# First layer, projections and the first maximum units of a two-layer graph kernel put into one pass

## The reference

```
h = max(layernorm(x), 0)
adj_hat = adj + I;  d = (rowsum(adj_hat) + 1e-8) ** -0.5
x = x + relu((d[:, None] * adj_hat * d[None, :]) @ h @ weight)      # layer 0

h = max(layernorm(x), 0)                                             # layer 1
q, k, v = (h @ W.T).reshape(128, 3327, 8) for W in (Wq, Wk, Wv)
a = einsum('dnh,dmh->dnm', q, k) * 128 ** -0.5 + adj + adj
out = einsum('dnm,dmh->dnh', softmax(a, axis=2), v).reshape(3327, 1024)
x = x + out @ Wo.T
```

## Time and profile before

| | us |
|---|---|
| median of 3 executions | 15108.52 (15092.42 to 15110.36) |
| the profiled execution, its own time | 15109.94 |
| its span, first to last instruction | 15108.1 |
| VectorE busy in the span | 13914.9 (92%) |
| TensorE busy | 13957.0 (92%) |
| ScalarE busy | 13462.3 (89%) |
| mean granted TensorE clock | 0.973 |

### The profile page before, as it was taken

One profiled execution on the slowest core, in us unless ns is written; L12 is line 12 of the kernel. 1 busy time (PEld: TensorE's weight loads), 2 busy tenths in 40 slices (PEclk: granted clock), 3 DMA queues, 4 the chain that ended last, 5 costly groups with the idle time before them and its releaser, 6 DMA issues. The chain is left out here.

```text
span 15108.1 us, 432848 instructions
## 1 busy us (share of the span) xinstructions
PE 13957.0 (92%) x143755; PEld 4993.4 (33%) x143755; DVE 13914.9 (92%) x27486; ACT 13462.3 (89%) x30436; POOL 336.0 (2%) x887
## 2 busy tenths in 40 slices
PE   1747999999999999999999999999999999999996
PEld 1612333333333333333333333333333333333334
DVE  3249999999999999999999999999999999999972
ACT  0225999999999999999999999999999999999993
POOL 0020000000000000000000000000000000000000
PEclk9867999999999999999999999999999999999996
DMA  7755565655656565655656565655656565655542
GB/s 282 228 129 123 135 143 134 138 138 136 139 135 143 133 144 134 141 134 134 143 134 144 133 141 134 143 134 134 144 134 141 134 143 135 143 135 137 139 108 59
DMA packets 2075487, 2120.62 MB, mean 140 GB/s; under 512 B 818858, under 2 KB 1827761, under 8 KB 2063377
## 3 DMA queue, kind: packets, MB, share of 16 engines
q1 hardware_dynamic: 2069616, 2049.07, 56.1%
q10 hardware_dynamic: 3744, 44.30, 0.7%
HBM read 1927.37 MB, written 165.28 MB: 139 GB/s over the span
## 5 line engine op out<-in xcount | busy, mean ns | idle before, releaser
L927 DVE CUSTOM_DVE_ANT_0 X<-X,adj_row 128x832 f32<-128x832 f32 x13312 | 13304.5, 1048 | 93.1 <-PE X L961 49.6
L866 ACT ACTIVATE prob<-S 128x416 f32<-128x416 f32 x26624 | 11894.9, 517 | 386.1 <-PE S L983 201.0
L983 PE MATMUL S<-q_blk,k_res 52*128 52x416 f16 x26624 | 6865.5, 343 | 44.5 <-ACT S L855 11.1
L1004 PE MATMUL O<-prob,v_pad 128*32 128x208 f32 (+1 forms) x87376 | 6721.1, 388 | 2.6
L961 PE MATMUL X<-mk,mq 40*128 40x416 f16 x26624 | 6298.9, 346 | 369.5 <-DVE m_part L927 335.3
L983 PEld LDWEIGHTS S<-q_blk,k_res 52*128 52x128 f16 x26624 | 2216.7, 93 | 4256.1 <-ACT S L855 1457.9
L1004 PEld LDWEIGHTS O<-prob,v_pad 128*32 128x32 f32 x87376 | 1830.0, 108 | 2531.8 <-issue 2048.0
L961 PEld LDWEIGHTS X<-mk,mq 40*128 40x128 f16 x26624 | 1586.7, 93 | 2434.5 <-DVE m_part L927 1999.8
L855 ACT ACTIVATE S<-adj_key 128x416 f32<-128x416 f32 x3328 | 1752.7, 527 | 184.0 <-DMA adj_key<-adj_by_key 148.7
L927 DVE DVE_READ_ACCUMULATOR2_ANT m_part<- 128x1 f32 x13312 | 1876.8, 141 | 0.0
L350 PE MATMUL tr<-ident,row 128*128 128x128 f32 x676 | 106.4, 286 | 322.8 <-DVE hn L300 321.7
(11 more groups left out here) (90 smaller groups left out, 1458.0 us busy)
## 6 DMA issues: line engine op xcount, KB each, us to landing
adj_row<-adj_padded SPq DMA_DIRECT2D x1664, 416.0 KB, 3.9
adj_key<-adj_by_key SPq DMA_DIRECT2D x3328, 208.0 KB, 3.4
mk<-k_planes SPq DMA_DIRECT2D x1664, 104.0 KB
mk<-k_planes SPq DMA_DIRECT2D x1664, 52.0 KB
adj_padded<-row ACTq DMA_DIRECT2D x26, 1664.0 KB, 5.4
row<-adj_padded SPq DMA_DIRECT2D x26, 1664.0 KB, 7.8
adj_by_key<-aT SPq DMA_DIRECT2D x26, 1664.0 KB, 11.9
row<-in_adj SPq DMA_DIRECT2D x25, 1663.5 KB, 7.3
```

The lines of the kernel that those rows point to most:

```text
L866: nc.scalar.activation(prob[c % QR][:, d % 4, :], S[b][:, 0:WB], ACT.Exp, scale=2.0).then_inc(s_e[b], 1)
L927: nc.vector.tensor_tensor_reduce(out=x_, in0=x_, in1=adj_row[gi % 4][:].rearrange("p (a b) -> p a b", a=2), scale=1.0, scalar=LOW, op0=ALU ...
L983: nc.tensor.matmul(S[b][:, 0:WB], k_res[base:base + KR, d // 2, s * P:(s + 1) * P], q_blk[n % 2][base:base + KR, d // 2, :], start=False, ...
L1004: done = nc.tensor.matmul(O[32 * d:32 * d + 32, cols], v_pad[:, s, 4 * q + d, :], prob[born(j, q) % QR][:, d, cols], start=first, stop=Tru ...
```

## The change

- Block 1 and block 2 become one block with one pass over the row tiles, and it also runs the first EU = 160 maximum units, eight in each of the row tiles 4 to 23, one or two in each group of transposes (`units_at`).
- The degree pass goes from the last tile to the first, with RB = 3 row buffers. Nothing but columns 2496 to 3327 (the fourth piece of `max_bias`) is stored, to `adj_tail`. The last three tiles loaded stay for the pass; the others are loaded from adj a second time.
- In the pass, tile t is transposed and aggregated while tile t - 1 is updated, normed (`row_update`, `row_norm`, `row_turn`) and projected (`project`, `rest`). `pj` is one bank; each half of q, k and v passes through it in turn. q, k and v have two buffers each in SBUF.
- `max_bias` reads adj itself for the first three pieces and `adj_tail` for the fourth, and only the rows there are: 127 in the last tile.
- In block 3 ScalarE and GpSimd fill parts of `k_res`, ScalarE's queue issues the first group's value loads after its fill, and 24 maximum units precede the first score. The maximum helpers are unchanged otherwise, and so are the cycles, the spans and the output block.

```diff
+    EU = 160
+    XT = 4
+    RB = 3
-    adjp_t = dram("adj_padded", (NP, NP), fp32)
+    tail_t = dram("adj_tail", (NP, 2 * XC), fp32)
...
+            def max_bias(sp, x, gi):
+                c, t = gi // 2, gi % 2
+                r0 = x * 256 + t * P
+                n = min(P, N - r0)
+                src = adj[r0:r0 + n, c * 2 * XC:(c + 1) * 2 * XC] if c < 3 else adj_tail[r0:r0 + n, :]
+                sp.dma_start(adj_row[gi % 4][0:n], src).then_inc(s_ar[gi % 4], 16)
...
+                def units_at(t, g):
+                    if t < XT or t >= XT + EU // 8:
+                        return []
+                    u = 8 * (t - XT) + g + (g > 3)
+                    return [u, u + 1] if g == 3 else [u]
...
+                        for i in range(NT):                      # SP, degree pass
+                            t = NT - 1 - i
+                            if i >= RB:
+                                wait(sp, s_deg, i - RB + 1)
+                                wait(sp, s_tl[i % RB], 16 * (i // RB))
+                            load(t, False)
...
+                        for t in range(NT + 2):                  # SP, the pass
+                            if 1 <= t and t - 1 + RB < NT:
+                                ...
+                                load(t - 1 + RB, True)
+                            if 1 <= t <= NT:
+                                ...
+                                sp.dma_start(adjT_cols[:, :, (t - 1) * P:t * P], aT[(t - 1) % 2][:]).then_inc(s_at[(t - 1) % 2], 16)
+                            if t >= 2:
+                                ...                              # q, k and v of tile t - 2
...
+                        wait(sp, s_res, 2 * NT)
+                        sp.dma_start(x1_rows, xs[:]).then_inc(s_xo, 16)
+                        wait(sp, s_xo, 16)
...
+                        def project(t, i, h):                    # ScalarE
+                            e, s, cols = t - 1, (t - 1) % 2, slice(512 * h, 512 * h + 512)
+                            act.wait_ge(s_pj, 6 * e + 2 * i + h + 1)
+                            if i < 2:
+                                ...
+                                first = nc.scalar.activation((q_parts, k_parts)[i][s][:, 0, cols], pj[:], ACT.Copy)
+                                if i == 1:
+                                    first.then_inc(s_hi, 1)
+                                else:
+                                    nc.scalar.activation(q_parts[s][:, 2, cols], pj[:], ACT.Copy, scale=-1.0).then_inc(s_ng, 1)
+                            else:
+                                ...
+                                nc.scalar.activation(v_out[s][:, cols], pj[:], ACT.Copy).then_inc(s_vc, 1)
...
+                        for t in range(NT + 1):                  # VectorE
+                            for g in range(GN):
+                                ...                              # its copy of a transposed group
+                                if t >= 1:
+                                    if g == 2:
+                                        row_update(t - 1)
+                                    if g == 3:
+                                        row_norm(t - 1)
+                                    if g == 4:
+                                        row_turn(t - 1)
+                                    if g in (4, 5):
+                                        rest(t - 1, g - 4, 0)
+                                        rest(t - 1, g - 4, 1)
+                                for u in units_at(t, g):
+                                    sweep(dve, u)
...
+                        for t in range(NT + 1):                  # TensorE
+                            for g in range(GN):
+                                ...                              # transposes of group g
+                                if t >= 1 and g >= 4:
+                                    project(t, g - 4, 0)
+                                for u in units_at(t, g):
+                                    maximum(pe, 0, u, 1, END * NG)
+                                    maximum(pe, 0, u, 0, END * NG)
+                                if g == 0 and t >= 1:
+                                    products(t - 1, GN - 1)
+                                elif g and t < NT:
+                                    products(t, g - 1)
+                                ...
+                                if t >= 1 and g >= 4:
+                                    project(t, g - 4, 1)
...
+                        for r0, r1 in PIECES:                    # ScalarE, block 3
+                            nc.scalar.activation(k_res[32:64, :, r0 * P:r1 * P], zero.unsqueeze(2).to_broadcast((32, GH // 2, (r1 - r0) * P)), ACT.Copy, bias=MAX_STEP).then_inc(s_kz[0], 1)
+                        act.wait_ge(s_vz, 3)
+                        for piece in range(len(PIECES)):
+                            group_values(act, 0, piece)
...
-                    for u in range(LEAD):
-                        maximum(0, u, 1, END * NG)
-                        maximum(0, u, 0, END * NG)
+                        for u in range(EU, LEAD):
+                            maximum(pe, 0, u, 1, END * NG)
+                            maximum(pe, 0, u, 0, END * NG)
```

More of the change, by code:

```diff
@@ L529, in graph_layers_kernel @@
-        with ExitStack() as c4:
-            sb, pb, sem = open_(c4)
-            k_res = sb("k_res", [P, GH // 2, NP], fp16)
-            q_blk = [sb(f"q_blk{i}", [P, GH // 2, WB], fp16) for i in range(2)]
+        with ExitStack() as shared:
+            sb, pb, sem = open_(shared)
             mq = [sb(f"mq{i}", [P, GH, 2 * P], fp16) for i in range(3)]
@@ new lines, in sweep @@
+            def sweep(dve, v):
+                xh, u = v // 64, v % 64
+                gi, d = u // 8, u % 8
+                c, t = gi // 2, gi % 2
+                if d == 0:
+                    dve.wait_ge(s_ar[gi % 4], xh * 32 + 16 * (gi // 4 + 1))
+                dve.wait_ge(s_x[u % 2], xh * 32 + (u // 2 + 1))
+                x_ = X[u % 2][:, :, 0:XC]
+                nc.vector.tensor_tensor_reduce(out=x_, in0=x_, in1=adj_row[gi % 4][:].rearrange("p (a b) -> p a b", a=2),
+                                               scale=1.0, scalar=LOW, op0=ALU.add, op1=ALU.max,
+                                               accum_out=m_part[xh % 2][:, c, GH * t + d:GH * t + d + 1]).then_inc(s_t, 1)
+                if u == 1 and xh:
+                    max_reduce(dve, xh - 1)
+                if u == 6 and xh:
+                    max_turn(dve, xh - 1)
@@ new lines, in maximum @@
+            def maximum(pe, k, u, rg, end):
+                if u >= end:
+                    return
+                c, t, d = u // 16, u // 8 % 2, u % 8
+                x = u // 64
+                if rg == 1:
+                    if u % 64 == 0:
+                        pe.wait_ge(s_mq[x % 3], k * (64 * 13) + 64 * (x // 3 + 1))
+                    if u % 16 == 0:
+                        pe.wait_ge(s_mk[c % 3], k * (64 * 52) + 64 * (c // 3 + 1))
+                    if u >= 2:
+                        pe.wait_ge(s_t, k * SPAN + (u - 1))
+                base = 64 * rg
+                done = nc.tensor.matmul(X[u % 2][:, rg, 0:XC], mq[x % 3][base:base + XR, d, t * P:(t + 1) * P], mk[c % 3][base:base + XR, d, :], start=True, stop=True)
+                if rg == 0:
+                    done.then_inc(s_x[u % 2], 1)
```

1498 lines of the change are left out of this document (728 added, 770 removed).

## The result

The changed kernel takes 15162.17 us (median of 7 executions, 15151.7 to 15170.23), the kernel before 15110.36 (7 executions). The ratio is 1.0036, with a 95% interval from 1.0024 to 1.0048: slower by 52 us. I had forecast 14983 and faster. The profiled execution took 15170.23 us, its span is 15168.2, and its mean granted clock 0.968.

A forecast was written before the change was run, and what follows sets the result against it. The maximum units, with VectorE nearly full in the long stage, were taken to bound it. 15109.9 - 409 (early stages) + 25 (hand-over) + 257 (edge-row stalls) = 14983 us; range 14,690 to 15,230.

The forecast's parts named there:

- unit 160 runs at: Start of maximum unit 160, after which the schedule is unchanged except loads: 863 us instead of 1272, a gain of 409.
- hand-over, loss: Before the first scores: ScalarE's fill and 24 value loads delay its biases to 53 us, needed at 27.5; loss 25.
- edge rows, loss of 16 groups: Long stage: 127-row `adj_row` loads of the last tile stall VectorE 16 us a head group, 257 us in all.
- 4S + 3R + 2 = 89.5 us, wanted at 49 + 24.4 = 73.4: Landing of a head group's fourth 127-row load against its use, 24.4 us being the prefetch depth: 16 us late.
- R: Usual work per 16 units of the DMA engine carrying the 127 rows: 6.5 us taken, bounds 5 and 7.7.
- S = 17: Time in us of one 127-row load on one DMA engine, taken between estimates of 16 and 18.5.
- (b): Long stage: same queue, slower, 24 us or more a group; 25.7 gives 15,137, 34 gives 15,270 us; chance 0.18.
- (a): Long stage: the 127-row loads are hidden, no stall; 14726 us (14,640 to 14,830); chance 0.21.
- (c): Pass over row tiles stays at 1.2 GHz, 37 us a tile: 15,248 us with the stalls, 14,991 without; chance 0.08.
- Degree pass: First stage: two loads in flight, 6.2 us a tile, so TensorE starts at 188 us (bounds 150 and 220) against 321.4.
- The pass over the tiles: Merged row-tile pass: limited by `pj`'s chain of product, copies and rest; 26 us a tile with units, 655 in all.
- Odd pitch "at nothing": Row loads of the maximum units from adj, whose rows are 3327 elements: the odd pitch costs nothing.

The follow-up runs named there:

- experiments 1 to 4: Changed kernel's 127-row loads: split 112+15, 14705.32 us; 113+14, 15014.92; 122+5, 14701.87; 97+30, 14850.12; half the columns, 14704.99. Kernel before with 127-row loads: 15550.92.
- experiment 6: Changed kernel with the four 127-row loads of a head group issued whole from ScalarE's queue instead of SP's: 15174.25 us, ratio 1.0041.
- 113 rows: Changed kernel with each 127-row load of the last row tile split into 113 and 14 rows: 15014.92 us, ratio 0.9934.
- 97 rows: Changed kernel with each 127-row load of the last row tile split into 97 and 30 rows: 14850.12 us, ratio 0.9832.
- 112 + 15: Changed kernel with each 127-row load of the last row tile split into 112 and 15 rows: 14705.32 us, ratio 0.9729.
- experiment 5: Kernel before, first three column pieces read from adj at its odd pitch, all loads with 128 rows: 15109.52 us, ratio 1.0002.
- experiment 2: Kernel before, with only its last row tile's load cut from 128 to 127 rows, still from the padded copy: 15550.92 us, ratio 1.0289.

## Why the prediction was wrong, point by point

The terms, predicted and found; the last column is what each adds to 14983.

| term | predicted | found | difference |
|---|---|---|---|
| unit 160 runs at | 863 | 836 | -27 |
| hand-over, loss | 25 | 41.4 | +16 |
| edge rows, loss of 16 groups | 257 | 457 | +200 |

The sum is 15,172, against 15,170.2 of the profiled execution; with the 464 that the ratios give for the edge rows it would be 15,179.

**The step that failed** is the price of the edge rows, "4S + 3R + 2 = 89.5 us, wanted at 49 + 24.4 = 73.4: VectorE stalls 16 us a group". The mechanism was right: 127 rows ride on one engine (experiments 1 to 4), the stall lies where it was said, in three pieces at the end of each group. The size was too small, by 12.6 us a group, and from 24.7 us a group on the change is a loss: what it gains elsewhere is 1272 - 836 = 436 us, less the 41 of the hand-over, over 16. Two things make up the 12.6:

- **R, "I take 6.5", the other work of that engine.** From 97 to 127 rows the fourth load comes later by 97.6 - 82.3 = 15.3 us, so a row costs 15.3 / 30 / 4 = 0.128 us and 127 rows 16.2: S = 17 was close. The rest of the 97.6 is 32.8 = 3R + 2, so R is 10.3, above both bounds of the sum (5 and 7.7). I had left out half of `adj_row`'s part of the packet share (7.7) and gone lower still for packet time that counts waiting (6.5); not even the whole share, 9.5, was enough. Nor is it SP's order: in experiment 6, where each load was issued before the one ahead was down, the four landings (27.9, 20.2, 26.5, 25.3 us) leave 35.0 us beside 4 x 16.2. Of that 11.7 lie ahead of the first load, where the formula had 2, so "R" also holds work that was queued before the first. Which transfers the engine served in those 33 to 35 us no run resolves; that part of the cause stays open. R is what the formula leaves, from one group in each kernel. It gives 97.6 - 73.4 = 24.2 us late, and the waits up to the fourth load do add to 24.4.
- **The time after the stall.** The loss is 28.6 a group, 4.4 more than 24.2. The formula ends when the fourth load is down; VectorE then goes on waiting for TensorE in pieces of 0.6 to 1.3 us, 2.6 in the group shown, at a granted clock of 0.57 from 1576 to 1586. The other 1.8 lie between one group and the mean of 16 and are not traced. With 113 rows, late by 16.9, the loss is 19.4 and 2.3 us of such waits follow; with 97 rows, late by 8.9, it is 9.1, and none follow.

**Rivals.** (b), "the same queue with the rates of the load rows", is what happened: 25.7 us a group and 15,137 by its first figures. It reached the size with too high an S (18.5) and too low an R (7.7). It had 0.18 because I held the lower R against it: "with VectorE stalled the other loads thin out". The DMA share did fall, to 0.31, and it didn't help. (a), hidden, is false, and its price of 14,726 is close to what 112 + 15 gives (14,705). (c) is false: the pass had a clock of 0.96.

**Degree pass.** Right: 188 forecast, 186.5 found.

**The pass over the tiles.** The mechanism was right: VectorE stands in `rest`, and what it waits for is ScalarE's copies out of `pj`, 125.5 us in the 400 us from 300 to 700, some 7.8 a tile; the granted clock was 0.96, near full. A tile with units takes 24.2 us where I took 26, 36 us less over the 20. The rest of the pass took 11 more than forecast, and with the 1.5 of the degree pass that is the 27.

**Hand-over.** ScalarE's part was right in kind: its issues ended at 898.5, 65.9 us after its fill began (832.6 in its timeline), where I had 53. The fill was shorter than forecast, 11.6 us against 13.8 (it has 13,312 elements a partition, not 13,824), the issuing longer, 59.8 against 38.4. What I had not costed is the row load for unit 184: it stands behind 24 key loads on DMA engines that were full, and the two waits, 21.4 and 17.9, came one after the other.

**Odd pitch "at nothing".** Right (experiment 5), and so the one number that mattered in `max_bias` was n.

## What to carry to other kernels

A last tile that is one row short is not one row cheaper: look at how its row count divides before the transfer's bytes, and split a count that has no divisor up to 16 (127 into 112 + 15), which here was worth 457 of 15162 us. When a cheap stage is shortened at the price of a transfer in the long stage, the loss is multiplied by the number of groups, so its error bars decide the sign: measure it alone, in the kernel before, as experiment 2 did. For a queue with one server, price from above what stands between the late transfers and ahead of the first, and add the time that the engines need to get back into step.

## What the runs showed of the hardware

- One DMA engine moved 3.3 KB rows at 0.128 us each, 26 GB/s, by the landings with 97 and 127 rows; in the middle of such a load the trace has a DMA share of 0.07 and 27 GB/s. By that, 127 of them took 16.2 us where a row load lands in a median of 3.6.
- A load on one engine holds up the queue behind it at issue: SP's next issue took 5.95 and 11.52 us, against 0.34 behind the 112 + 15 rows. With the loads on ScalarE's queue SP's issues behind the first three were short, behind the fourth one took 14.47 us for two loads, and the time was the same.
- The issue time says little where the engines are full: with a DMA share over 1 a whole row load took 25.8 us to land.
- With stalls of 3 to 9 us that come 24 and 30 us apart TensorE's granted clock was 0.79 over 65 us, and back at 1.00 in the next 32.
